# Second expert layer's up products as three fp32r products each, with split weights and activations

## The reference

```python
def _L0_ffn_ref(x, router_w, router_b, w1, b1, w2, b2, sw1, sb1, sw2, sb2):
    xf = x.reshape(-1, d_)
    probs = jax.nn.softmax(xf @ router_w + router_b, axis=-1)
    tw, ti = jax.lax.top_k(probs, K)                 # K = 8 of E = 64
    tw = tw / jnp.sum(tw, axis=-1, keepdims=True)
    def body(acc, p):
        W1, B1, W2, B2, e = p                        # W1 is 128 x 32
        h = jax.nn.silu(xf @ W1 + B1) @ W2 + B2
        cw = jnp.sum(jnp.where(ti == e, tw, 0.0), axis=-1)
        return (acc + cw[:, None] * h, None)
    routed, _ = jax.lax.scan(body, jnp.zeros_like(xf), (w1, b1, w2, b2, jnp.arange(64)))
    def shared_mlp(W1, B1, W2, B2):                  # two of them, 128 x 256
        return jax.nn.silu(xf @ W1 + B1) @ W2 + B2
    shared = jnp.sum(jax.vmap(shared_mlp)(sw1, sb1, sw2, sb2), axis=0)
    return (routed + shared).reshape(b_, s_, d_)
```

## Time and profile before

| | us |
|---|---|
| median of 3 runs | 1420.85 |
| all three runs | 1420.2, 1420.85, 1595.93 |
| the profiled execution's own time | 1419.12 |
| its span, first to last instruction | 1417.3 |
| mean granted clock of PE | 0.887 of full |

### The profile page before, as it was taken

How to read it: one execution, slowest core, us unless ns; L and a number is a source line. 1 busy time by engine, 2 the same in 40 slices (tenths; PEclk the granted TensorE clock), 3 DMA queues, 4 the chain that set the end, 5 groups by cost and what they waited for, 6 DMA issues and landing times.

```text
span 1417.3 us, 13196 instructions
## 1 busy us (share of the span) xinstructions
PE 1098.8 (78%) x3858; PEld 574.3 (41%) x3858; DVE 975.5 (69%) x2190; ACT 714.4 (50%) x1368; POOL 614.4 (43%) x426
## 2 busy tenths in 40 slices
PE   3225968787887878688877776868986899999796
PEld 1002323332332333333333534535553556556565
DVE  5965788678866886477667787656645535549787
ACT  7505663476437653443433524434562358746564
POOL 1970787158733965022023573454433131225222
PEclk8556989988998989589898989989998999999898
DMA  6000000000000000200001000000000200000000
GB/s 213 0 0 1 0 1 0 1 0 0 0 1 1 0 1 13 89 0 0 1 14 53 1 0 1 1 1 0 1 1 1 67 0 1 8 1 8 0 8 8
DMA packets 11271, 17.76 MB, mean 13 GB/s; under 512 B 1304, under 2 KB 7584, under 8 KB 10688
## 3 DMA queue, kind: packets, MB, share of 16 engines
q1 hardware_dynamic: 11200, 16.93, 3.6%
HBM read 15.88 MB, written 1.05 MB: 12 GB/s over the span
## 4 chain that ended last, share of the span: by engine, by line
PE 38%; DVE 11%; ACT 7%; POOL 3%; issue 3%; POOLq 0%; DVEq 0%; ACTq 0%
PE bankE L1833 6%; PE bankE L1218 3%; ACT b_pr L1116 2%; PE bankS L1796 2%; PE bankE L1750 2%; PE bankE L1280 2%; PE bankS L1750 2%; PE bankS L1781 2%; PE bankS L1753 1%; PE bankE L1239 1%; PE bankE L615 1%; PE bankE L1753 1%; PE bankS L1723 1%; PE bankE L575 1%; PE bankE L608 1%
## 5 line engine op out<-in xcount | busy, mean ns | idle before, releaser
L727 DVE TENSOR_TENSOR_SCAN hs<-dA,carry,bankS 128x512 f32<-128x512 f32 x128 | 156.7, 1265 | 3.2
L331 POOL TENSOR_TENSOR hc<-hs,cb 128x1024 f32<-128x1024 f32 x56 | 131.9, 2356 | 35.1 <-DVE hs L727 32.3
L306 POOL TENSOR_TENSOR cv<-cv,hc 128x1024 f32<-128x1024 f32 x56 | 132.1, 2358 | 4.4
L1708 ACT ACTIVATE c_h<-bankE,C 128x512 f32<-128x512 f32 x144 | 98.7, 687 | 52.4 <-PE bankE L1833 50.1
L1602 POOL TENSOR_TENSOR c_acc<-c_acc,c_tw 128x512 f32<-128x512 f32 x32 | 46.0, 1436 | 159.1 <-DVE c_tw L1927 159.0
L439 ACT ACTIVATE sg<-bankE,C 128x512 f32<-128x512 f32 x80 | 54.9, 687 | 82.5 <-PE bankE L575 82.4
L719 DVE TENSOR_TENSOR bankS<-dx,bankS 128x1024 f32<-128x1024 f32 x64 | 78.3, 1223 | 6.7 <-PE bankS L504 6.1
L1833 PE MATMUL bankE<-c_fH,c_w1H 128*128 128x512 f32 x144 | 80.9, 562 | 1.1 <-ACT c_h L1708 1.1
L392 ACT ACTIVATE dA<-dl,Aneg 128x512 f32<-128x512 f32 x128 | 80.2, 708 | 0.1
L615 PE MATMUL bankE<-hh,f 128*128 128x512 f32 x128 | 70.4, 631 | 10.3 <-DVE hh L837 10.3
L538 PE MATMUL bankE<-h2T,wg 128*128 128x512 f32 x128 | 72.1, 646 | 3.5 <-ACT sg L420 1.4
(11 more groups left out here) (516 smaller groups left out, 2877.8 us busy)
## 6 DMA issues: line engine op xcount, KB each, us to landing
c_w<-in_w SPq DMA_DIRECT2D x1, 2304.0 KB, 8.7
X<-in_x SPq DMA_DIRECT2D x4, 256.0 KB, 4.1
wg<-in_gate_T SPq DMA_DIRECT2D x1, 1024.0 KB, 7.5
wu<-in_up_T SPq DMA_DIRECT2D x1, 1024.0 KB, 9.5
f<-in_w SPq DMA_DIRECT2D x1, 1024.0 KB, 7.2
out<-X SPq DMA_DIRECT2D x4, 256.0 KB, 2.3
b_wq<-in_Wqkv SPq DMA_DIRECT2D x1, 768.0 KB, 4.4
g<-in_sw SPq DMA_DIRECT2D x2, 256.0 KB, 3.4
```

What stands on the lines that cost most here:

```text
L306: pool.tensor_tensor(cv[:, :, :], cv[:, :, :], (hv if by_vector(i, k) else hc)[:, :, :], ALU.add).then_inc(s["y_acc"], 1)
L331: pool.tensor_tensor(dst[:, :, :], hs[:, k % HS, :, :], cb[:, k % 2, :].unsqueeze(1).to_broadcast([P, HV, G]), ALU.mult).then_inc(s["hc_re ...
L727: V.tensor_tensor_scan(hs[:, k % HS, h, :], dA[:, (HV * k + q) % DA, :], dbx[:, h, :], carry[:, k, h:h + 1], ALU.mult, ALU.add).then_inc(s ...
L1708: act.activation(h[:, n % 3, :], E[k % 2][:, :], ACT.Gelu_apprx_tanh, bias=col("b1_3", k)).then_inc(s["fs_ready"], 1)
```

## The change

The up products of U0 to U19 are no longer one fp32 product each. Weights and activations are each split into a high part rounded to fp32r and a low part, the rest; each block is then high x high + low x high + high x low, three fp32r products that accumulate in the same bank.

- Weights, once: five new pieces aS0 to aS4 (128 x 512 each) stand in the order after aF0.1, before aF7.1. ACT copies w to the high part, POOL subtracts to get the low part, which is written over w.
- Activations, per group, in piece L5: ACT copies bank E[1] a second time, to fH; DVE, which had nothing to do in L5, waits for that and subtracts, giving fL. fH lies over xnE and fL over yT.
- PE waits for both at U0.
- The places of the SBUF regions move down by 7168 bytes to make room; the scratch of software DMAs shrinks from 8192 to 1024. The semaphores of the last layer's splits are shared with the new ones (names change, instructions do not).

```diff
-MAMBA_END = 125920
-KL_END = 116320
-WINDOW_END = 184000
+MAMBA_END = 118752
+KL_END = 109152
+WINDOW_END = 176832
...
-... aF1.1 aF5.1 aM0.0 aF6.1 aF2.1 aF0.1 aF7.1 aM1.0 aF3.1 ...
+... aF1.1 aF5.1 aM0.0 aF6.1 aF2.1 aF0.1 aS0.0 aS1.0 aS2.0 aS3.0 aS4.0 aF7.1 aM1.0 aF3.1 ...
...
     f1 = sb2("f1", [P, E1N * H1])
+    f1L = second_lane.over_last("f1L", [P, E1N * H1], F32R)
+    f1H = sb2("f1H", [P, E1N * H1], F32R)
...
     xnE = sb2("xnE", [P, G])
+    fH = second_lane.over_last("fH", [P, G], F32R)
...
     yT = sb2("yT", [P, G])
+    fL = second_lane.over_last("fL", [P, G], F32R)
...
+    SPLIT = ((g1, g1H, g1L, 0), *((f1, f1H, f1L, k) for k in range(4)))
...
# gpsimd
+            if p[0] == "S":
+                w, high, low, part = SPLIT[k]
+                pool.wait_ge(s["w1_high"], k + 1)
+                pool.tensor_tensor(low[:, part * G:(part + 1) * G], w[:, part * G:(part + 1) * G], high[:, part * G:(part + 1) * G].bitcast(F32), ALU.subtract).then_inc(s["w1_low"], 1)
...
# scalar
+            if p[0] == "S":
+                w, high, low, part = SPLIT[k]
+                if k == 0:
+                    act.wait_ge(s["ld_e"], 160)
+                act.activation(high[:, part * G:(part + 1) * G], w[:, part * G:(part + 1) * G], ACT.Copy).then_inc(s["w1_high"], 1)
...
                 act.activation(fT[:, :], E[1][:, :], ACT.Copy).then_inc(s["fT_ready"], 1)
+                act.activation(fH[:, :], E[1][:, :], ACT.Copy).then_inc(s["fHL"], 1)
...
# tensor
-                w = f1[:, b * P:(b + 1) * P] if b >= 0 else g1[:, k * P:(k + 1) * P]
-                pe.matmul(E[k % 2][:, :], w, fT[:, :], start=True, stop=True).then_inc(s["up_ready"], 1)
+                wH, wL, c = (f1H, f1L, b) if b >= 0 else (g1H, g1L, k)
+                if k == 0:
+                    pe.wait_ge(s["w1_low"], 5)
+                    at_least(pe, s["fHL"], e, 2, 2)
+                for q, (wp, fp) in enumerate(((wH, fH), (wL, fH), (wH, fL))):
+                    mm = pe.matmul(E[k % 2][:, :], wp[:, c * P:(c + 1) * P], fp[:, :], start=(q == 0), stop=(q == 2))
+                mm.then_inc(s["up_ready"], 1)
...
# vector
+            elif p == "L5":
+                at_least(V, s["fHL"], e, 2, 1)
+                V.tensor_tensor(fL[:, :], E[1][:, :], fH[:, :].bitcast(F32), ALU.subtract).then_inc(s["fHL"], 1)
...
-SBUF = (8320, 229368)
-SCRATCH = 8192
+SBUF = (1152, 229368)
+SCRATCH = 1024
```

More of the change, by code:

```diff
@@ L99 @@
     aN9.0 aA7.0 an9.0 ao9.0 aN10.0 an10.0 ao10.0 aN11.0 an11.0 ao11.0 aN12.0 an12.0 ao12.0 aN13.0 an13.0 ao13.0 aN14.0 an14.0 ao14.0 aN15.0
-    an15.0 ao15.0 aB1.0 aB3.0 aB4.0 aB2.0 aF1.1 aF5.1 aM0.0 aF6.1 aF2.1 aF0.1 aF7.1 aM1.0 aF3.1 aF8.1 aR1.0 aF9.1 aA0.1 aR3.0 aA1.1
+    an15.0 ao15.0 aB1.0 aB3.0 aB4.0 aB2.0 aF1.1 aF5.1 aM0.0 aF6.1 aF2.1 aF0.1 aS0.0 aS1.0 aS2.0 aS3.0 aS4.0 aF7.1 aM1.0 aF3.1 aF8.1 aR1.0 aF9.1 aA0.1 aR3.0 aA1.1
     aR4.0 aN0.1 an0.1 aM2.0 ao0.1 aN1.1 aM3.0 an1.1 aM4.0 aA2.1 ao1.1 aN2.1 an2.1 aM5.0 ao2.1 aM6.0 aA3.1 aN3.1 an3.1 aM7.0 ao3.1 aN4.1
@@ L165, in mamba_and_experts @@
     g1 = sb2("g1", [P, SB1 * P])
+    g1L = second_lane.over_last("g1L", [P, SB1 * P], F32R)
+    g1H = sb2("g1H", [P, SB1 * P], F32R)
     g2 = sb2("g2", [P, SB1, D])
@@ L293, in piece @@
             k = int(p[1:])
-            if p == "F1":
+            if p[0] == "S":
+                w, high, low, part = SPLIT[k]
+                pool.wait_ge(s["w1_high"], k + 1)
+                pool.tensor_tensor(low[:, part * G:(part + 1) * G], w[:, part * G:(part + 1) * G], high[:, part * G:(part + 1) * G].bitcast(F32), ALU.subtract).then_inc(s["w1_low"], 1)
+            elif p == "F1":
                 power("f_var", "f_pow", powF, rsF, i, 0, 2)
@@ L349, in piece @@
             k = int(p[1:])
-            if p == "F6":
+            if p[0] == "S":
[3 more added lines that the diff above has]
+                act.activation(high[:, part * G:(part + 1) * G], w[:, part * G:(part + 1) * G], ACT.Copy).then_inc(s["w1_high"], 1)
+            elif p == "F6":
                 at_least(act, s["xhT_ready"], i, 1, 1)
@@ L1649, in piece @@
                 w, high, low = (t_[:, k * FF3:(k + 1) * FF3] for t_ in (w1, w1H, w1L))
-                pool.tensor_copy(high, w).then_inc(s["c_split"], 1)
-                pool.wait_ge(s["c_split"], k + 1)
-                pool.tensor_tensor(low, w, high.bitcast(F32), ALU.subtract).then_inc(s["c_w1"], 1)
+                pool.tensor_copy(high, w).then_inc(s["w1_high"], 1)
+                pool.wait_ge(s["w1_high"], 5 + k + 1)
+                pool.tensor_tensor(low, w, high.bitcast(F32), ALU.subtract).then_inc(s["w1_low"], 1)
             elif p[0] == "s":
@@ L1827, in piece @@
                 if i == 0 and f == 0:
-                    pe.wait_ge(s["c_w1"], x_ + 1)
+                    pe.wait_ge(s["w1_low"], 5 + x_ + 1)
                 if k == 0:
-                    pe.wait_ge(s["c_fHL"], 2 * i + 2)
+                    pe.wait_ge(s["fHL"], 2 * NG + 2 * i + 2)
                 for q, (wp, fp) in enumerate(((w1H, fH), (w1H, fL), (w1L, fH))):
@@ L1998, in piece @@
                 f_, fh, fl = fT[:, i % 2, :], fH[:, i % 2, :], fL[:, i % 2, :]
-                dve.tensor_copy(fh, f_).then_inc(s["c_fHL"], 1)
-                dve.wait_ge(s["c_fHL"], 2 * i + 1)
-                dve.tensor_tensor(fl, f_, fh.bitcast(F32), ALU.subtract).then_inc(s["c_fHL"], 1)
+                dve.tensor_copy(fh, f_).then_inc(s["fHL"], 1)
+                dve.wait_ge(s["fHL"], 2 * NG + 2 * i + 1)
+                dve.tensor_tensor(fl, f_, fh.bitcast(F32), ALU.subtract).then_inc(s["fHL"], 1)
                 dve.wait_ge(s["lg_ready"], 2 * NG + i + 1)
```

## The result

The changed kernel takes 1430.85 us (median of 4 runs, 1429.08 to 1432.13), the kernel before beside it 1420.67 (4 runs): a ratio of 1.007, 95% interval 1.0058 to 1.0082. That is 10.2 us more, where 7.1 were forecast; 1428.0 was predicted. One of the four runs of the kernel before took 1595.93 us, as one of e5_both's twelve took 2761.97; the ratios leave such a run out, and without it the median before is 1420.49 (e5_both's 1417.85). The profiled execution has a span of 1429.3 us (before: 1417.3), 12.0 more.

The account below looks back on a forecast made before the run. DVE was taken to bound the second expert layer in the first three groups, PE only in group 3. Costs 2.5 + 0.1 + 2.5 + 2.7 + 2.4 = 10.2, less 3.1, gave 7.1 more: 1428.0 us, range 1419 to 1438.

Parts of the forecast that it names:

- The price: PE's up products: three fp32r products take 0.70 us at full clock where one fp32 product takes 0.86.
- the loop of group 3: Second expert layer, group 3: still 2.19 us a block, as the up product runs in the shadow of hh.
- The gain on the path: Of 12.8 us of PE time saved by shorter up products, 3.1 us reaches the path, between 2 and 5.
- Rival 1: PE is the bound wherever busy: all 12.8 us count, costs only 5.4, time falls to 1413.5; chance 0.08.
- the forecast's split into 1.4, 1.2 and 0.5: Gain by place: 1.4 us in group 3's chain, 1.2 at stage ends before the next projections, 0.5 at stage starts.
- 8 x 0.16: Stage ends, groups 0 to 2: two or three up products per group before the next projections, given as 1.2 us.
- Steps of the track: L5: DVE's new wait for fH delays it 2.5 us in group 0, 0.1 in 1, 2.5 in 2, 2.7 in 3.
- The convolution was to end 2.4 us late: Start of Mamba group 1: DVE's last three convolution instructions stand behind POOL's subtractions, 2.4 us, bounds 1.0 and 3.8.
- the 7.1 of the sum: Whole kernel: costs of 10.2 us less a gain of 3.1 make it 7.1 us slower.
- Nothing absorbs this: L5, groups 0 and 2: the 2.5 us delay counts whole, since DVE bounds the stage and POOL waits for its scans.
- rival 3: PE's clock stays at half through the second expert layer: at least 30 us more, 1451, over 2% slower; chance 0.03.
- Rival 2: DVE's two-input instructions collide more with POOL's, up to 1.8 us each, three per group: up to 1440 or 1445; chance 0.12.

Follow-up runs that it names:

- e5_both: Changed kernel with DVE's fL subtraction moved to the router piece R2 and the weight splits moved (ACT's into group 0's Mamba steps, POOL's behind the convolution): 1417.98 against 1421.26.
- e3_fp32_up: Changed kernel with all splits and waits, but the up product one fp32 product of the high weights: 1434.67 against 1421.77 for the kernel before.
- e6_both_fp32: e5_both with one fp32 up product of high weights and whole activations instead of three fp32r products: 1420.42 against 1421.26 for the kernel before.
- e10: Kernel before plus only the activation halves fH, fL and their waits, up product still fp32, no weight split: 1429.42 against 1421.36.
- e9: Kernel before plus only the weight split, one fp32 up product of the high weights, no activation halves: 1424.16 against 1421.36.
- e2: Changed kernel with ACT's weight copies moved among group 0's Mamba steps and POOL's subtractions behind the convolution: 1428.53 against 1421.77 for the kernel before.
- e1: Changed kernel with DVE's fL subtraction moved from L5 to the head of router piece R2: 1420.8 against 1421.77 for the kernel before.
- e4_same_again: The changed kernel run once more, nothing edited: 1431.02 against 1421.77 for the kernel before.
- e12: e10 plus a pure delay of six repeated instructions, 3.1 us, in the convolution of Mamba group 1: 1437.06 against 1420.4 for the kernel before.

## Why the prediction was right, and what it missed

**PE's product.** The price held: 0.70 for three. So did the loop of group 3, 2.21 for 2.19. The gain on the path was forecast at 3.1 within 2 to 5 and is 3.8 (e3_fp32_up less the changed kernel) or 2.4 (e6_both_fp32 less e5_both). Rival 1, all 12.8 us, is out. Where in the stage the gain lies, the forecast's split into 1.4, 1.2 and 0.5, was not tested; its 8 x 0.16 is 1.3.

**L5.** Steps of the track, predicted and measured (changed kernel; e10 in brackets): group 0 2.5, 2.4 (2.4); group 1 0.1, 0.0 (0.0); group 2 2.5, 2.4 (2.4); group 3 2.7, 2.4 (2.1). The chain of reasons is in the rows: DVE's wait 2.98 us where "about 3" was said, the router's own wait gone, L876 still beside POOL's L343, POOL's L298 down to 1.01. With fL taken out of L5 the steps vanish. Alone the four cost 8.1 us by the medians (7.8 forecast), but that agreement is partly luck: e10's four steps sum to 6.9, and the rest of its track is rises and falls where the change has no instruction, 2.8 at 516.5 the largest.

**aS0 to aS4.** The mechanism was right, and the sum nearly so by two errors that cancel. The convolution was to end 2.4 us late and is 3.05 longer, since each of its instructions and each of POOL's suffers (L305 has a median of 1.71 us where the earlier trace rows have 1.27); but xc's first half is used early, so PE's product starts 3.8 later, of which this execution was 1.8 behind already: 2.0. Then this product takes 1.7 more, of which 0.35 is given back in a shorter wait: 3.3 in all. By medians it is 2.8 alone (e9), 2.3 beside the waits of L5 (the changed kernel less e2), 2.8 beside the late fL (e1 less e5; 2.3 when each is taken against its own kernel before). That two-input instructions of DVE and POOL's take turns is also what the Trainium skill says (SBUF — State Buffer, Who interferes with whom); by that rule the trace agrees, with 7.10 us for 4.05 on DVE and 1.71 for 1.27 on POOL.

**The term that was missing.** The forecast's terms at their measured size give 2.8 + 8.1 - 3.8 = 7.1, the 7.1 of the sum, and the kernel costs 9.3 to 10.2. The 2 to 3 us between are the step that failed: "Nothing absorbs this" was as far as the working went for the delays, which were then added as they are. The place of that error is shown by the tracks; its size isn't, as each of these medians is good to some 2 us only, and as 2.8 and 8.1 hold some of the clock's share already. I had priced the clock only as a catastrophe for a whole stage (rival 3, 30 us), not as a product or two behind each new wait. Its mechanism was the right one at a tenth of the size: group 2 loses 2.6 us behind L5 that way, the product of xc 1.3, and lane b gives 2.5 back. Rival 2, more collisions of DVE and POOL, has no part in it: the three router steps that it named (L850, L822, L826) have medians of 1.60, 0.86 and 1.39 us, and now (L876, L848, L852) of 1.68, 0.87 and 1.39.

**What stays open.** Why the traced shift of 3.7 us changes the low stretches at 280, 516 and 830 us and the traced ones of 1.6 and 7.3 don't, no run here tells. Chance of the execution may be part of it. At about 280 us the changed kernel's product of xc took 1.93 us in its first trace and 3.30 in e4_same_again, the same program, both after a wait of 0.3; e12's took 3.56 after 0.31, with no wait over 1.14 on PE in the 15 us before. So the wait right before a product is not the whole rule.

## What to carry to other kernels

Price a new wait twice: by how long it delays its engine, and by what PE then does behind it. If it makes PE wait for some 3 us where it had waited 1, and nothing covers the next product, add up to that product's time once more (1.5 to 1.8 us for 1.93 here). Copies and subtractions for a split product can be had for nothing that these runs could measure, but only where their engine has a slot and no one is queued behind the wait (0.0 to 0.1 us of track in e6_both_fp32); putting a subtraction one Mamba step later was worth 10 us here, about three times the gain that it served. And compare medians for the size and a track of two traces for the place: a single pair of executions had up to 3.5 us between them before the first changed instruction.

## What the runs showed of the hardware

- The product of xc in Mamba group 1: 1.93 us after waits of 0.89 to 1.08 us (5 traces), 3.42 to 3.70 after waits of 2.64 to 8.39 (7 traces); the next, 1.98 or 3.78. At the same product of group 2 a wait of 0.3 us went with 1.93 and with 3.3 to 3.6.
- A pure delay on the path of 1.6, 3.7 and 7.3 us cost 1.8, 5.5 and 11.8 (95% intervals 0.6 to 4.3, 3.8 to 8.7, 8.4 to 12.1).
- Six two-input DVE instructions beside GpSimd's subtractions: 7.10 us for 4.05; GpSimd's own went from 1.27 to a median of 1.71.
- Three fp32r products of 128x512 start 0.23 us apart at full clock, with each weight load (0.19) inside the product before it.
- The same instructions in different executions meet falls of PE's clock at different times: 0.0 to 3.5 us apart by 120 us, before any of them has a changed instruction (three had ScalarE's copies, which left no step).
